# One block for the whole program, and a head in two halves with the first projections made beside the decay sums

## What is computed

```python
x = x + attn0(layernorm(x))    # q,k,v: 32 heads, 8 kv; dt = softplus(x Win + b); G = cumsum(-exp(A) dt)
                               # y = (q k^T * exp(G_i - G_j)) (v dt) + state; y / rms * silu(x Wg); y Wo
x = x + ffn0(layernorm(x))     # softmax router over 64, top 8: x * sum(w) + w @ expert_bias
x = x + attn1(layernorm(x))    # x,B,C: conv over 4 tokens, silu; dt; 128 heads, 8 groups, decay sums; gate; out
x = x + ffn1(layernorm(x))     # router over 64, top 16; rank-16 adapters A, B
```

## Time and profile before

| | us |
|---|---|
| median of 3 runs | 2567.82 |
| lowest, highest | 2565.51, 2568.74 |
| the profiled execution | 2562.39 |
| its span (first to last instruction) | 2560.7 |
| PE busy | 2473.7 (97%) |
| DVE, ACT, POOL busy | 71%, 58%, 60% |

### The profile page before, as it was taken

One profiled execution on the slowest core, in us unless ns is written; L12 is line 12 of the kernel. 1 busy time (PEld: TensorE's weight loads), 2 busy tenths in 40 slices (PEclk: granted clock), 3 DMA queues, 4 the chain that ended last, 5 costly groups with the idle time before them and its releaser, 6 DMA issues.

```text
span 2560.7 us, 53900 instructions
## 1 busy us (share of the span) xinstructions
PE 2473.7 (97%) x19326; PEld 2009.8 (78%) x19326; DVE 1827.8 (71%) x2688; ACT 1486.1 (58%) x3410; POOL 1540.6 (60%) x1495
## 2 busy tenths in 40 slices
PE   5999999999999888999999999999999999999989
PEld 4878788788887677787888788778878877887777
DVE  5776766767767778668778678587687786785864
ACT  3535535445354465666765775676667657756721
POOL 1654656546556332667767677686677676676810
PEclk8999999999999989999999999999999999999999
DMA  3230230312303024323322222222232223222111
GB/s 101 43 84 29 69 79 22 83 43 49 82 26 71 29 74 160 115 67 115 101 75 83 100 92 75 94 102 96 67 113 94 76 88 104 83 82 94 59 39 49
DMA packets 93549, 199.00 MB, mean 78 GB/s; under 512 B 11248, under 2 KB 19440, under 8 KB 93296
## 3 DMA queue, kind: packets, MB, share of 16 engines
q1 hardware_dynamic: 93296, 195.64, 24.8%
HBM read 184.46 MB, written 11.14 MB: 76 GB/s over the span
## 4 chain that ended last, share of the span: by engine, by line
PE 56%; DVE 2%; POOL 1%; issue 1%; DMA 0%; ACT 0%; SPq 0%; POOLq 0%; DVEq 0%; ACTq 0%
PE proj L210 13%; PE proj L212 12%; PE proj L211 12%; PE core_y L1633 5%; PE core_o L1639 3%; PE turned L245 1%; PE mx_decay L210 1%; PE mx_decay L212 1%; PE mx_decay L211 1%; PE core_y L212 1%; PE core_y L210 1%; PE core_y L211 1%; PE turned L1663 1%; PE mx_normed L1663 1%; PE mx_normed L245 1%; PE core_o L1673 1%
## 5 line engine op out<-in xcount | busy, mean ns | idle before, releaser
L210 PE MATMUL proj<-slab_hi,XTL 128*128 128x512 f32 x816 | 348.3, 427 | 1.0 <-DVE mx_gate L1853 0.4
L193 DVE TENSOR_TENSOR slab_lo<-slab_raw,slab_hi 128x512 fp32r<-128x512 f32 (+2 forms) x256 | 239.2, 946 | 118.7 <-ACT slab_hi L184 117.5
L212 PE MATMUL proj<-slab_hi,XTH 128*128 128x512 f32 x816 | 320.0, 392 | 0.0
L211 PE MATMUL proj<-slab_lo,XTH 128*128 128x512 f32 x816 | 319.0, 391 | 0.0
L210 PE MATMUL proj<-XTH,slab_lo 128*128 128x512 f32 x716 | 289.9, 405 | 25.0 <-PEq L81 7.4
L212 PE MATMUL proj<-XTH,slab_hi 128*128 128x512 f32 x716 | 282.6, 395 | 0.0
L211 PE MATMUL proj<-XTL,slab_hi 128*128 128x512 f32 x716 | 282.4, 394 | 0.0
L210 PE MATMUL proj<-slab_hi,mx_otl 128*128 128x512 f32 x576 | 240.5, 418 | 3.0 <-DVE mx_otl L259 3.0
L1921 POOL TENSOR_TENSOR mx_gate<-mx_gate,mx_hd 128x512 f32<-128x512 f32 x128 | 167.4, 1308 | 102.7 <-DVE mx_hd L1824 91.9
L904 POOL TENSOR_TENSOR at_ropeA<-at_ropeA,at_ropeB 128x512 f32<-128x512 f32 x80 | 110.5, 1381 | 195.0 <-DVE at_ropeB L840 195.0
L212 PE MATMUL proj<-slab_hi,mx_oth 128*128 128x512 f32 x576 | 227.7, 395 | 0.0
(11 more groups left out here) (415 smaller groups left out, 6672.7 us busy)
## 6 DMA issues: line engine op xcount, KB each, us to landing
mx_g_all<-sums SPq DMA_DIRECT2D x128, 512.0 KB, 3.7
at_g_all<-sums SPq DMA_DIRECT2D x64, 256.0 KB, 8.1
slab_raw<-in_w_gate SPq DMA_DIRECT2D x64, 256.0 KB, 2.9
slab_raw<-in_w_out SPq DMA_DIRECT2D x64, 256.0 KB, 2.8
slab_raw<-in_w_x SPq DMA_DIRECT2D x60, 256.0 KB, 4.7
slab_raw<-in_w_q SPq DMA_DIRECT2D x32, 256.0 KB, 2.8
slab_raw<-in_w_g SPq DMA_DIRECT2D x32, 256.0 KB, 2.9
slab_raw<-in_w_o SPq DMA_DIRECT2D x32, 256.0 KB, 5.3
```

Of the source, the lines that this page charges most:

```text
L193: op = nc.vector.tensor_tensor(K.SL[par][:, c, 0:width], K.RAW[c][:, 0:width], hi, ALU.subtract)
L210: nc.tensor.matmul(to[:, 0:bh.shape[-1]], al, bh, start=(c == 0), stop=False)
L211: nc.tensor.matmul(to[:, 0:bh.shape[-1]], ah, bl, start=False, stop=False)
L212: mm = nc.tensor.matmul(to[:, 0:bh.shape[-1]], ah, bh, start=False, stop=(c == KC - 1))
```

## The change

Everything after setup stands in one block, so the barriers between phases go; each phase still has a branch of its own on each engine. What they guarded is now guarded by waits: PE at the middle's start waits for at_x and xl_b, its mixer units for taps of the conv banks.

The head makes statistics and rstd of 4 tiles, then of the other 4; the dt unit of the first half of tokens is made after 4 tiles (bank PT), the second after k0 (bank PD). SP's slabs for k/v and w_q are loaded and split in the head (w_q's high and low parts ahead of the decay sums on ACT and DVE). k0, k1, v0 and v1 of the first round have banks of their own and don't wait for ropes; decay transposes and copies stand in slot 6. SP's rounds are written out.

The diff (lines that only follow from it are left out):

```diff
@@ -134,21 +126,24 @@
...
-        with ExitStack() as mem:
-            dt0, upto0, left0 = (mem.enter_context(nc.sbuf_tensor(n, [P, NT, H0], F32)) for n in ("dt0", "upto_sum0", "to_last0"))
-            with joined(nc, K):
-                norm_phase(nc, K, "a", d["w_dt0"], False)
-                decay_phase(nc, K, d, sums[0], dt0, [upto0, left0])
-            attention_phase(nc, K, d, sums[0], dt0, upto0, left0)
-        with ExitStack() as mem:
...
-            with joined(nc, K):
-                middle_phase(nc, K, d, sums[1], dt1, upto1, less1, from_start, to_end, bc_scratch)
-            mixer_phase(nc, K, d, sums[1], bc_scratch, dt1, upto1, less1, from_start, to_end, out)
+        with nc.Block() as K.block:
+            with ExitStack() as mem:
+                dt0, upto0, left0 = (mem.enter_context(nc.sbuf_tensor(n, [P, NT, H0], F32)) for n in ("dt0", "upto_sum0", "to_last0"))
+                with ExitStack() as K.mem:
+                    head_phase(nc, K, d, sums[0], dt0, upto0, left0)
+                attention_phase(nc, K, d, sums[0], dt0, upto0, left0)
...
+                K.GB = [mem.enter_context(nc.sbuf_tensor(f"mx_g_all{i}", [P, HH1, P], F32)) for i in range(4)]
+                K.tri = mem.enter_context(nc.sbuf_tensor("mx_tri", [P, P], F32))
...
+                with ExitStack() as K.mem:
+                    middle_phase(nc, K, d, sums[1], dt1, upto1, less1, from_start, to_end, bc_scratch)
+                mixer_phase(nc, K, d, sums[1], bc_scratch, dt1, upto1, less1, from_start, to_end, out)
...
+    def store_sums(sp):
...
-        sp.wait_ge(st, HEAD + 16 * NB)
-
-    @block.tensor
-    def _(pe):
-        pe.wait_ge(S["xl_a"], HEAD + NT)
-        for half in range(2):
-            unit(nc, K, pe, half, channel_parts(K, N % 2, 0, half), wait_slab=N)
+
+    def decay_turns(pe):
         for src, ready, bank in ((q, DT_READY, K.PT), (G, G_READY, K.PD), (R, R_READY, K.PO)):
...
+    def dt_unit(pe, half):
+        pe.wait_ge(xl, HEAD + Q4 * (half + 1))
+        at = slice(half * HALF, (half + 1) * HALF)
+        unit(nc, K, pe, DTB[half], lambda c: (WH[:, c, :], WL[:, c, :], K.XTH[:, c, at], K.XTL[:, c, at]), wait_slab=N)
...
+        pe.wait_ge(S["loaded2"], HEAD + 32)
+        for t in range(Q4):
+            turn(t)
+        dt_unit(pe, 0)
+        for t in range(Q4, NT):
+            turn(t)
+
+    @block.gpsimd
+    def _(pool):
+        for half in range(2):
+            a = slice(Q4 * half, Q4 * (half + 1))
+            pool.wait_ge(aggr, HEAD + Q4 * (half + 1))
+            alone(pool)
+            nc.gpsimd.tensor_scalar(ve[:, a], K.mv[:, a, 1], EPS, None, ALU.add).then_inc(rs, 1)
+            pool.wait_ge(rs, HEAD + 2 * half + 1)
+            alone(pool)
+            nc.gpsimd.tensor_tensor(K.rstd[:, a], ve[:, a], K.mhalf[:, a], ALU.pow).then_inc(rs, 1)
...
+        for c in range(KC):
+            act.wait_ge(K.raw_loaded[c], HEAD + 16 * (N + 1))
+            nc.scalar.activation(WH[:, c, :], K.RAW[c][:, 0:P], ACT.Copy).then_inc(K.hi_done, 1)
+        for t in range(Q4):
+            hi(t)
         act.wait_ge(ld, HEAD + 32)
         nc.scalar.activation(ea[:, :], alog[:, :], ACT.Exp).then_inc(av, 1)
+        for c in range(KC):
+            split_hi(nc, K, act, N + 1, (N + 1) % 2, c, 0, width=2 * D0)
+        for t in range(Q4, NT):
+            hi(t)
+        for c in range(KC):
+            split_hi(nc, K, act, N + 2, N % 2, c, 0)
         for b in range(NB):
-            act.wait_ge(K.unit_done, HEAD + U + b // 2 + 1)
+            act.wait_ge(K.unit_done, HEAD + (1, 1, 3, 3)[b])
             at = slice(b * H0, (b + 1) * H0)
-            nc.scalar.activation(z[at, :], K.PJ[b // 2][at, (b % 2) * SEQ:(b % 2 + 1) * SEQ], ACT.Identity,
+            nc.scalar.activation(z[at, :], DTB[b // 2][at, (b % 2) * SEQ:(b % 2 + 1) * SEQ], ACT.Identity,
...
+        nc.vector.memset(ones[:, :], 1.0)
+        for half, (sem, count) in enumerate((("loaded", 16), ("loaded2", 32))):
+            dve.wait_ge(S[sem], HEAD + count)
+            for t in range(Q4 * half, Q4 * (half + 1)):
+                stream_stats(nc, K, t, stats)
+            for t in range(Q4 * half, Q4 * (half + 1)):
+                tile_aggr(nc, K, dve, "a", t)
+        for t in range(Q4):
+            made(t)
+        lo(0)
+        for c in range(KC):
+            dve.wait_ge(K.hi_done, HEAD + KC * N + c + 1)
+            nc.vector.tensor_tensor(WL[:, c, :], K.RAW[c][:, 0:P], WH[:, c, :].bitcast(F32), ALU.subtract).then_inc(K.lo_done, 1)
+        for t in range(1, Q4):
+            lo(t)
+        for t in (4, 5):
+            made(t)
         first_lo(nc, K, dve, N + 1, 2 * D0)
+        for t in (6, 7):
+            made(t)
+        for t in range(Q4, NT):
+            lo(t)
+        first_lo(nc, K, dve, N + 2, SLAB)
         dve.wait_ge(av, HEAD + Z)
...
         PS = [K.PO, mem.enter_context(nc.psum_tensor("at_scores", [P, SLAB], F32))]
+        KV_FIRST = [PS[1], K.PJ[1], mem.enter_context(nc.psum_tensor("at_first_v", [P, SLAB], F32)), K.PY]
+
+        def bank(g, s):
+            return KV_FIRST[s] if g == 0 and s < 4 else K.PJ[s % 2]
...
                 for c in range(KC):
                     load_slab(sp, n + 1, 1, g, c)
+                if g == 0:
+                    K.store_sums(sp)
                 for c in range(KC):
                     load_slab(sp, n + 2, 2, g, c)
+                if g == 0:
+                    sp.wait_ge(S["dt_st_0"], HEAD + 16 * NB)
                 sp.wait_ge(S["at_e"], HEAD + PAIRS * g)
...
-            with sp.Fori(0, KV0 - 1) as g:
-                round_(g, False)
-            round_(KV0 - 1, True)
+            for g in range(KV0):
+                round_(g, g == KV0 - 1)
...
+                    if g == 0 and s == 6:
+                        pe.wait_ge(S["at_v"], HEAD + 2)
+                        K.decay_turns(pe)
                     pk, pi = units[s - 2]
                     back = NT if s < 2 else 0
-                    if pk == "k":
+                    if g == 0 and s < 5:
+                        if s == 0:
+                            pe.wait_ge(S["xl_a"], HEAD + 4)
+                        else:
+                            pe.wait_ge(S["xl_a"], HEAD + NT)
+                    elif g == 0 and s == 5:
+                        pe.wait_ge(S["at_ra"], HEAD + 2)
+                    elif pk == "k":
                         pe.wait_ge(S["at_ra"], HEAD + 10 * g + pi + 1)
                     elif pk == "v":
                         pe.wait_ge(S["at_vT"], HEAD + 2 * g + pi + 1)
...
                     if kind in "kv":
-                        unit(nc, K, pe, s % 2, channel_parts(K, slot, int(kind == "v"), i), wait_slab=w)
+                        unit(nc, K, pe, bank(g, s), channel_parts(K, slot, int(kind == "v"), i), wait_slab=w)
+                        if g == 0 and s == 0:
+                            K.dt_unit(pe, 1)
...
                     for j, c in split.get(s, []):
-                        hi(act, n, g, j, c, last)
+                        if g or j > 1:
+                            hi(act, n, g, j, c, last)
+                    if g == 0 and s == 6:
+                        K.decay_copies(act)
...
+def row_load(K, sp, sums, q, t):
+
+    sp.wait_ge(K.S["mx_e"], HEAD + 16 * q + 2 * t - 6)
+    sp.dma_start(K.GB[t % 4][:, :, :].rearrange("p h n -> p (h n)"), sums[t:t + 1, ds(HH1 * P * q, HH1 * P)]
+                 .broadcast_to([P, HH1 * P])).then_inc(K.S[f"mx_row{t % 4}"], 16)
+
...
-    SCAN_AT, Q_AT, G_AT, R_AT, STORE_AT = 14, 18, 22, 26, 15
+    SCAN_AT, Q_AT, G_AT, R_AT, STORE_AT = 14, 18, 24, 28, 15
...
     @block.sync
     def _(sp):
+        sp.wait_ge(S["at_y"], HEAD + NT * KV0)
         sp.dma_start(rbias[:, :], d["router_bias"]).then_inc(rld, 16)
-        for i in range(2):
-            sp.dma_start(EB[i * NE:(i + 1) * NE, :], d["expert_bias"]).then_inc(rld, 16)
         sp.dma_start(bias[:, :], d["dt_bias1"]).then_inc(ld, 16)
         sp.dma_start(alog[:, :], d["a_log1"]).then_inc(ld, 16)
         sp.dma_start(K.CW[:, :, :], d["conv_w"]).then_inc(S["bc_ld"], 16)
         sp.dma_start(K.CB[:, :], d["conv_b"]).then_inc(S["bc_ld"], 16)
+        sp.wait_ge(S["xnT_b"], HEAD + 4)
+        for i in range(2):
+            sp.dma_start(EB[i * NE:(i + 1) * NE, :], d["expert_bias"]).then_inc(rld, 16)
...
+            if u == ROWS_AT:
+                sp.dma_start(K.tri[:, :], d["tri"]).then_inc(S["mx_ld"], 16)
+                sp.dma_start(K.DB[:, :], d["D"]).then_inc(S["mx_ld"], 16)
+                sp.dma_start(K.NW[:, :], d["norm_w"]).then_inc(S["mx_ld"], 16)
+                sp.wait_ge(st, HEAD + 16)
+                for t in range(4):
+                    row_load(K, sp, sums, 0, t)
...
+        pe.wait_ge(S["at_x"], HEAD + NT * KV0 - 1)
+        pe.wait_ge(S["xl_b"], HEAD + 4)
...
-        XB = [K.PJ[0], PD[1], K.PJ[1], K.PY, PD[1], K.PJ[0], K.PJ[1], K.PY]
+        XB_FIRST = [PD[1], K.PJ[0], K.PJ[1], K.PY, PD[1], K.PJ[0], K.PJ[1], K.PY]
```

(10 more changed lines are left out.)

184 lines of the change are left out of this document (69 added, 115 removed).

## The result

The changed kernel takes 2545.54 us (median of 4, 2542.43 to 2549.08), the kernel before beside it 2566.66 us (2562.76 to 2568.74): a ratio of 0.9922, 95% interval 0.9911 to 0.9934, 21 us less. Timed once more later, it took 2543.61 us against 2565.28: 0.9925, 0.9911 to 0.9938. The prediction was 2546.8, with 2540 to 2556 as its range.

A forecast was written before the change was run, and what follows sets the result against it. PE was taken as the bound, busy 2473.7 of 2560.7 us, so only its 87.0 us of idle time could be won. Terms 10.5 + 1.5 + 9.0 = 21.0 us off the median 2567.8 gave 2546.8, range 2540 to 2556.

The forecast's parts named there:

- The head: From the start to q2 in the first attention round: 10.5 us gained, bounds 7.8 and 12.7.
- Attention to middle: Crossing to the router units: 1.5 us gained through alog's earlier load, bounds 0.2 and 2.2.
- Inside the middle: G's transposes moved from conv unit 22 to 24, with 3.60 us of PE idle time there: priced at nothing.
- upper end of my range: Most gain, all places: 12.7 + 2.2 + 11.5 = 26.4 us, 2541.4, said to hold G's 3.60; chance 0.04.
- Middle to mixer: Crossing up to the mixer's fifth x unit: 9.0 us gained, bounds 5.9 and 11.5.
- my lower bound of 5.9: Crossing from middle to mixer: the least gain in us, DVE's gain alone.
- the first rival: Unit 24: moved row loads delay stores that ACT's conv starts wait for; 4.8 us lost, 2551.6; chance 0.10.
- The sum: All places together: 10.5 + 1.5 + 9.0 = 21.0 us gained, 2546.8 on the median; chance 0.66.
- the branch that stays for each phase: Three phase crossings: up to 0.96 us of instruction fetch might stay at each, giving 2549.7; left out of the sum.
- w_q's split: Head, ahead of the decay sums: late w_q chunks hold ACT and DVE; 4 us lost, 2550.8; chance 0.10.
- The early start: First attention round: the head's gain is lost again, only 10.5 us gained elsewhere, 2557.3; chance 0.06.
- SP's written-out rounds: SP queue, 8 rounds: falls behind by 5.3 us each, 42.4 in all, 2589.2; chance 0.04.

The follow-up runs named there:

- e7: Changed kernel with PE waiting for the end of the decay sums before k1, v0 and v1; 2546.79 us in one execution.
- e3: Changed kernel with the barriers between attention and middle and between middle and mixer put back; 2552.67 us (median of 4), ratio 0.9955 to the kernel before.
- e5: Changed kernel with the transposes of the decay sums put back to conv units 22 and 26 from 24 and 28; 2544.89 us in one execution.
- e1: Changed kernel with the first four row loads put back behind the last store of B and C, without a barrier; 2546.88 us in one execution.
- e2: Changed kernel with the first four row loads spread over conv units 17, 18, 22 and 23 instead of all at 24; 2541.36 us in one execution.
- e8: Changed kernel with SP's rounds 2 to 7 in a hardware loop again; 2542.82 us in one execution.
- e4: Changed kernel with ACT's two copies of v moved ahead of k's high part in the first round; 2544.22 us in one execution.
- e9: Changed kernel with DVE's ropes of k0 and k1 moved from behind the decay sums into its two waits there; 2542.87 us in one execution.
- e11: Changed kernel with the edits of e9 and e2, and w_g's loads issued ahead of the stores of the sums; 2537.08 us in one execution.
- e12: The kernel of e11 timed against the kernel before: 2535.22 us against 2565.28, ratio 0.9884.

## Why the prediction was right

**The head** was right step by step; the steps came 0.4 to 1.2 us sooner than I had laid them out: first product 12.14 (12.5), dt unit 0 at 17.85 (18.3), first step of the sums 29.27 (30.1), their end 37.06 (37.9), v's transposes 42.38 (43.05), PE's pause 5.97 (6.2), q2 51.31 (52.5). POOL's sum took 1.26 and not 1.73. The term of 10.5 measured 11.7 at q2 and 12.7 at the attention's end. The name I gave to it, work in the shadow of the sums, is the smaller part: by e7 it is 2.4 us of it.

**Attention to middle**: 1.5 predicted, 14.5 - 12.7 = 1.8 measured, for the reason given: the second router unit at 868.09 still waits 2.05 us for DVE's lows, and the whole chain to it is earlier since ACT doesn't stand for alog. By e3 a barrier there takes 2.9 us back, 1.8 of them the barrier's.

**Inside the middle**: G's move was priced at nothing, and e5 shows nothing that is clear of the scatter. (The upper end of my range was to hold its 3.60 us; the sum 12.7 + 2.2 + 11.5 doesn't have them. And PE's last matmul of the middle ends at 1014.81, not 1014.65.) But my sum had DVE's last taps keep their place relative to the router, and they did not: the last silu gained 11.2 us where the choice of experts had gained 14.5, so 3.3 us were lost in between.

**Middle to mixer** is the term that was mis-sized: 9.0 predicted, 19.6 - 14.5 = 5.1 measured (5.8 in the second profile of the changed kernel), below my lower bound of 5.9. That bound was DVE's gain alone with the last taps in their place, and they came late. The cause is the first rival, which I gave 0.10 and 4.8 us: the row loads hold the stores, ACT waits 4.21 us for one. e1 takes the wait away, e2 takes it away and keeps the early rows, and gets up to 5.0 us back; in e2 the crossing gives 10.1, and by the table 8.4. I argued against it that few stores stand behind the loads. What counts is that ACT's four buffers come free by these stores: unit 29's convolution start, the one that waited, needs the store of unit 25, and that is the first one behind the loads. The number of stores behind it didn't matter. The Trainium skill ("DMA: Bandwidth & Descriptors", "Queues, rings and completion order") says that each DMA engine takes the descriptors of a ring in their order. The trace agrees, with 4.21 us where the loads stand ahead of that store and, in e1, no such wait where they stand behind it.

**The sum** of 21.0 was 19.6 at the fifth x unit, 18.2 at the last group, 16.5 at the end of the profiled executions, and 21 between the medians. The head gave 2.2 more than predicted, the mixer 3.9 less. The hit is in part two errors that cancel.

**The other rivals.** w_q's split didn't hold the sums: at 29.27 DVE had waited 2.36 us for z, which waited for PE. The early start wasn't lost in the rounds. SP's written-out rounds cost nothing (e8). Of the branch that stays for each phase, nothing shows: PE's first idle time behind the attention is 1.17 us at 862.47, released by DVE, and PE goes from the head to k0 (22.43) and from the last conv unit to the first x unit (994.36) without idle time. The Trainium skill ("Runtime: NRT & Kernel Launch", "Instruction fetch mechanics") says that a branch out of what is already fetched has to wait for the fetch; at these three places the trace of PE shows no such time, where the prediction had up to 0.96 us for each.

## What to carry to other kernels

When a barrier goes, its own microsecond is the small part; ask which work may now pass it, and put only what is waited for into the queues there. Transfers that are moved early belong where the same queue's next entries aren't awaited: here the same 2 MB made an engine wait 3.4 to 4.5 us when issued at one conv unit, and 1.2 to 2.4 us when spread over the units ahead, at a place where it waits up to 1.1 us without them. And behind a pause that an edit removes, follow two waits further, not one: e4, e7 and e9 each moved a pause and kept a part of it.

## What was not expected of the hardware

**DVE beside POOL.** In e9 the same 128x256 step took 0.43 us with POOL idle and 1.35, 1.55, 1.40 and 1.40 with POOL at a product or difference of 128x512, and ended when POOL did or close to it (29.27 + 1.35 = 30.62 against POOL's 30.33; 34.56 + 1.55 = 36.11 against 35.82). The ropes, which read one of their inputs from PSUM, kept their 0.69 us beside POOL (at 40.31 in the changed kernel, POOL working from 39.72 to 40.98). The Trainium skill ("Advanced Engine Details and Errata", "GPSIMD Details") says that POOL shares a read and a write interface with DVE and conflicts with DVE instructions that have two inputs in SBUF. The trace agrees.

**Two speeds of the first dt unit.** It starts at 17.6 to 18.0 in the twelve profiles that have the head of the changed kernel up to there, behind a pause of PE of 1.45 to 1.68 us. In seven of them its first matmul takes 0.50 us and the next ones 0.40; in five 0.80 and 0.63, as in this one:

```profile
17.80 0.80 PE L205 MATMUL turned<-XTH,hd_dt_lo 128*128 128x512 f32 x1 [1.45 <-DVE XTL L494]
...
18.40 0.63 PE L206 MATMUL turned<-XTL,hd_dt_hi 128*128 128x512 f32 x1
```

and the decay sums then start at 30.6 to 31.3 instead of 29.0 to 29.3, whatever the kernel (e2, e3, e4, e11 and e12 are the five).
